# Low rank A of the down projection as extra columns of its weights, and a later place for each tile's last low rank product

## The reference, cut to what matters

```
def _qlinear(x, q, scale, A, Bm):            # I = 1376, H = 512, R = 32
    w = (q.astype(jnp.float32) - 7.5) * (scale * 0.005)[:, None]
    y = jnp.einsum('bsh,oh->bso', x, w)
    return y + 0.02 * (x @ A @ Bm)
g = _qlinear(x, gate_q, gate_scale, gate_A, gate_B)
u = _qlinear(x, up_q, up_scale, up_A, up_B)
h = jax.nn.silu(g) * u
return _qlinear(h, down_q, down_scale, down_A, down_B)   # the map this change is about
```

## Time and profile before

| | |
|---|---|
| device time, three runs | 394.75 us median (393.98 to 395.04) |
| profiled execution | 394.56 us, of which the span of instructions 392.5 us |
| TensorE busy | 381.8 us (97%), 1967 records |
| DVE, ACT, POOL busy | 242.6 us (62%), 174.2 us (44%), 80.2 us (20%) |
| DMA | 40.5 MB, 103 GB/s in the mean |
| chain that ended last | TensorE 86%, DVE 4%, DMA 3%, ACT 3% |
| of it L560; L545; L543 | 37%; 21%; 5% |

### The profile page before, as it was taken

How to read it: one execution, slowest core, us unless ns; L and a number is a source line. 1 busy time by engine, 2 the same in 40 slices (tenths; PEclk the granted TensorE clock), 3 DMA queues, 4 the chain that set the end, 5 groups by cost and what they waited for, 6 DMA issues and landing times.

```text
span 392.5 us, 5221 instructions
## 1 busy us (share of the span) xinstructions
PE 381.8 (97%) x1967; PEld 292.6 (75%) x1968; DVE 242.6 (62%) x370; ACT 174.2 (44%) x307; POOL 80.2 (20%) x67
## 2 busy tenths in 40 slices
PE   8999999999999999999999999999999999999894
PEld 3776787678888876788888767888887778996341
DVE  2649888746376663463766634638889542546994
ACT  6436698312355653123556531235567310575122
POOL 2001433321122232121222321212323312000000
PEclk9899999999999999999999999999999999999999
DMA  7897574199500000072000000860000699790235
GB/s 215 260 287 256 187 225 144 43 343 153 68 1 0 2 0 0 6 116 40 3 0 2 2 0 2 123 142 2 0 0 3 186 291 243 127 224 0 82 135 214
DMA packets 81960, 40.47 MB, mean 103 GB/s; under 512 B 52344, under 2 KB 72840, under 8 KB 81808
## 3 DMA queue, kind: packets, MB, share of 16 engines
q1 hardware_dynamic: 69280, 37.80, 36.7%
q10 hardware_dynamic: 12480, 1.56, 2.9%
q0 software_dynamic: 176, 0.79, 0.7%
HBM read 26.38 MB, written 13.75 MB: 102 GB/s over the span
## 4 chain that ended last, share of the span: by engine, by line
PE 86%; DVE 4%; DMA 3%; ACT 3%; issue 1%; SPq 1%; POOL 0%; DVEq 0%; ACTq 0%
PE ps L560 37%; PE ps L545 21%; PE ps L543 5%; PE ps L570 5%; PE ps L589 4%; PE ps L710 3%; PE ps L505 3%; DMA stage_sel<-in_sel 2%; PE ps L691 2%; PE ps L591 2%; DMA lr_b_rows<-lr_b_parts 1%; PE ps L620 1%; PE ps L519 1%; PE ps L594 1%; PE ps L466 1%
## 5 line engine op out<-in xcount | busy, mean ns | idle before, releaser
L911 POOL TENSOR_TENSOR h_lo<-a_buf,h_hi 128x512 fp32r<-128x512 f32 (+1 forms) x44 | 57.5, 1308 | 143.4 <-ACT h_hi L810 143.4
L560 PE MATMUL ps<-x_hi,gate_w 128*128 128x512 f32 (+1 forms) x176 | 69.8, 397 | 0.1
L560 PE MATMUL ps<-x_hi,up_w 128*128 128x512 f32 (+1 forms) x176 | 69.7, 396 | 0.1
L560 PE MATMUL ps<-x_lo,gate_w 128*128 128x512 f32 (+1 forms) x176 | 69.5, 395 | 0.0
L545 PE MATMUL ps<-down_w,h_hi 128*128 128x512 f32 (+1 forms) x176 | 69.4, 394 | 0.0
L545 PE MATMUL ps<-down_w,h_lo 128*128 128x512 f32 (+1 forms) x176 | 69.3, 394 | 0.0
L560 PE MATMUL ps<-x_lo,up_w 128*128 128x512 f32 (+1 forms) x176 | 69.3, 394 | 0.0
L1155 DVE TENSOR_TENSOR a_buf<-a_buf,b_buf 128x512 f32<-128x512 f32 (+1 forms) x44 | 54.2, 1233 | 11.7 <-ACT a_buf L860 9.8
L846 ACT ACTIVATE a_buf<-ps,gate_sc 128x512 f32<-128x512 f32 (+1 forms) x44 | 30.2, 686 | 27.8 <-POOL h_lo L911 25.5
L1150 DVE TENSOR_TENSOR b_buf<-ps,b_buf 128x512 f32<-128x512 f32 (+1 forms) x44 | 30.1, 685 | 18.7 <-ACT b_buf L849 14.5
L849 ACT ACTIVATE b_buf<-ps,up_sc 128x512 f32<-128x512 f32 (+1 forms) x44 | 30.1, 684 | 23.4 <-PE ps L560 23.3
(11 more groups left out here) (172 smaller groups left out, 491.5 us busy)
## 6 DMA issues: line engine op xcount, KB each, us to landing
x_nat<-in_x SPq DMA_DIRECT2D x4, 1024.0 KB, 7.3
out<-x_nat SPq DMA_DIRECT2D x16, 256.0 KB, 2.3
turned<-x_nat SPq DMA_DIRECT2D x12, 256.0 KB, 3.3
x_nat<-in_down_q SPq DMA_DIRECT2D x11, 256.0 KB, 3.0
x_nat<-in_gate_q SPq DMA_DIRECT2D x10, 256.0 KB, 7.1
x_nat<-in_up_q SPq DMA_DIRECT2D x10, 256.0 KB, 8.4
edges<-zeros SPq DMA_DIRECT2D x4, 512.0 KB, 9.5
xt<-turned SPq DMA_DIRECT2D x6, 256.0 KB, 3.5
```

Source lines behind the costliest of these rows:

```text
L560: last = mm(ps[0:k, bank(ic, 2 * m), :], w[:, H * ic + c * k:H * ic + (c + 1) * k], part[:, c, :], start=c == 0 and part is x1_hi, stop=c ...
L911: nc.gpsimd.tensor_tensor(h_lo[0:k, ic, :], a_buf[0:k, ic % 2, :], plain(h_hi[0:k, ic, :]), ALU.subtract).then_inc(h_lo_ready, 1)
```

## The change

`down_w` gets a second axis: two halves of 256 weight columns, each followed by 32 columns of A, the high part of A in the first half and the low part in the second. Each product of the down map is made twice, once for each half, with 288 moving columns, into two banks: 4 and 5 for even groups, 6 and 7 for odd ones. The products of L543, `down_a_w`, `pd`, the selecting product and the semaphores of these go.

The low rank intermediate now comes out per group, not turned: 128 tokens x 32, in two banks. DVE's `down_scaled` adds both parts in a reduction of 4 x 32 x 2 values (the 32 sums, four times side by side) into `s4`, and then scales the two halves into `y_buf`. `down_turn` turns `s4` on TensorE, a float32 product of 128 columns with the identity, into the odd bank of the pair; ACT (`down_high`) and DVE (`down_low`) split it, scaled, into the group's 128 columns of `t4d`. The low rank product then goes to the even bank of the pair. Both stand in the next group: the turning product at step 2, the low rank one at step 6; in a last group that has the conditioning ahead of it at steps 0 and 8. For a tile's last group the turning product stands behind the next tile's L620 products, the low rank one behind its selecting products (whose banks become 1 and 3 except in tile 0); for the very last group they stand behind convolutions 0 and 1. `down_sum` moves accordingly, and ACT's stores of the last tile stand between its `down_high` steps.

```diff
-        down_w = sb("down_w", [P, IC, H], F32R)
+        down_w = sb("down_w", [P, IC, 2, HALF + R], F32R)
-        pd = sb("pd", [P, TILE], F32R)
+        s4 = sb("s4", [P, 2, P], F32)
...
+        def sel_bank(t, m):
+            return bank(1 if t == 0 else 0, 2 * m + 1)
...
-            def down_repeat(t):
-                pe.wait_ge(pd_hi_ready, t + 1)
-                pe.wait_ge(pd_lo_ready, t + 1)
-                mm(ps[:, 7, :], sel[:], pd[:], start=True, stop=True).then_inc(seld_mm, 1)
+            def down_turn(t, j):
+                n = t * TG + j
+                pe.wait_ge(s4_ready, n + 1)
+                pe.wait_ge(yq_ready, n + 1)
+                mm(ps[:, 5 + 2 * (j % 2), 0:P], s4[:, n % 2, :], ident[:], start=True, stop=True).then_inc(turn_mm, 1)
             def down_low_rank(t, j):
-                if j == 0:
-                    pe.wait_ge(t4d_hi_ready, t + 1)
-                    pe.wait_ge(t4d_lo_ready, t + 1)
-                mm(ps[:, 6 + j % 2, :], t4d[:, j * P:(j + 1) * P], down_b4[:],
+                n = t * TG + j
+                pe.wait_ge(t4d_hi_ready, n + 1)
+                pe.wait_ge(t4d_lo_ready, n + 1)
+                mm(ps[:, 4 + 2 * (j % 2), :], t4d[:, j * P:(j + 1) * P], down_b4[:],
                    start=True, stop=True).then_inc(down_l_mm, 1)
+            def mixed_between(t, j):
+                return j == TG - 1 and t + 1 < TILES
...
-                    if j == 1 and ic == 3:
-                        down_repeat(t)
-                    if j == 1 and ic == 8:
-                        down_low_rank(t, 0)
+                    if j > 0 and ic == (0 if mixed_between(t, j) else 2):
+                        down_turn(t, j - 1)
+                    if j > 0 and ic == (8 if mixed_between(t, j) else 6):
+                        down_low_rank(t, j - 1)
                     for part in (h_hi, h_lo):
-                        if j == 0:
-                            low = mm(ps[0:2 * R, 6, :], down_a_w[0:k, ic].rearrange("p m r -> p (m r)"),
-                                     part[0:k, ic, :], start=first, stop=end)
-                        last = mm(ps[:, 4 + j % 2, :], part[0:k, ic, j * P:(j + 1) * P], down_w[0:k, ic, :],
-                                  start=first, stop=end)
+                        for m in range(2):
+                            last = mm(ps[:, 4 + 2 * (j % 2) + m, 0:HALF + R], part[0:k, ic, j * P:(j + 1) * P],
+                                      down_w[0:k, ic, m, :], start=first, stop=end)
                 last.then_inc(down_mm, 1)
-                if j > 0:
-                    down_low_rank(t, j)
...
+                    if t > 0 and c == HC - 1:
+                        down_turn(t - 1, TG - 1)
...
+                for m in range(2):
+                    mm(ps[:, sel_bank(t, m), :], sel[:], pa[m], start=True, stop=True).then_inc(sel_mm, 1)
                 if t > 0:
-                    pe.wait_ge(y_ready, t * TG)
-                for m in range(2):
-                    mm(ps[:, bank(1, 2 * m + 1), :], sel[:], pa[m], start=True, stop=True).then_inc(sel_mm, 1)
+                    down_low_rank(t - 1, TG - 1)
+                    pe.wait_ge(y_ready, t * TG - 1)
...
                     if t > 0:
+                        if m == 1:
+                            pe.wait_ge(y_ready, t * TG)
                         quantised(t, 1, m)
...
                 convolve(n)
+                if n == 0:
+                    down_turn(TILES - 1, TG - 1)
+                if n == 1:
+                    down_low_rank(TILES - 1, TG - 1)
...
-            def down_high(t):
-                act.wait_ge(seld_mm, t + 1)
-                activation(t4d[:], ps[:, 7, :], copy).then_inc(t4d_hi_ready, 1)
+            def down_high(t, j):
+                n = t * TG + j
+                act.wait_ge(turn_mm, n + 1)
+                activation(t4d[:, j * P:(j + 1) * P], ps[:, 5 + 2 * (j % 2), 0:P], copy,
+                           scale=LR_SCALE).then_inc(t4d_hi_ready, 1)
...
-                for j in range(TG):
-                    if j == 0:
-                        down_high(t)
+                for j in range(TG - 1):
                     if j == 2 and t < TILES - 1:
                         split_mixed(t + 1)
-            for g in range(LATE, GROUPS):
...
+                    down_high(t, j)
+                    if t == TILES - 1 and j > 0:
+                        act.wait_ge(x2_ready, LATE + j)
+                        store(act, LATE + j - 1, stored_late)
+            down_high(TILES - 1, TG - 1)
+            act.wait_ge(x2_ready, GROUPS - 1)
+            store(act, GROUPS - 2, stored_late)
+            act.wait_ge(x2_last, 1)
+            store(act, GROUPS - 1, stored_late)
...
             def down_scaled(t, j):
                 n = t * TG + j
+                x = 4 + 2 * (j % 2)
                 dve.wait_ge(down_mm, n + 1)
                 if n >= 2:
                     dve.wait_ge(x2_ready, n - 1)
-                v.tensor_tensor(y_buf[:, j % 2, :], ps[:, 4 + j % 2, :], down_sb[:], ALU.mult).then_inc(yq_ready, 1)
+                    dve.wait_ge(turn_mm, n - 1)
+                both = ps[:, x:x + 2, HALF:HALF + R].rearrange("p m r -> p r m").unsqueeze(1).to_broadcast([P, P // R, R, 2])
+                v.tensor_reduce(s4[:, n % 2, :].rearrange("p (c r) -> p c r", r=R), both, AX_X, ALU.add).then_inc(s4_ready, 1)
+                v.tensor_tensor(y_buf[:, j % 2, :].rearrange("p (m n) -> p m n", m=2), ps[:, x:x + 2, 0:HALF],
+                                down_sb[:].rearrange("p (m n) -> p m n", m=2), ALU.mult).then_inc(yq_ready, 1)
...
                 if t > 0:
                     x_a_low(t)
+                    down_low(t - 1, TG - 1)
+                    down_sum(t - 1, TG - 1)
```

More of the change, by code:

```diff
@@ L24 @@
 HC = H // P
+HALF = H // 2
 IC = -(-I // P)
@@ L282, in slot, with slot_values @@
             return x_nat[:, GROUPS - RING + n % RING, 0:slot_width(n)].bitcast(I32)
+        def slot_values(n):
+            return slot(n).rearrange("p (m n) -> p m n", m=2) if slots[n][0] == "down" else slot(n)
         def slot_dram(n):
@@ L290, in slot_weights @@
             kind, ic = slots[n]
-            w = {"gate": gate_w[:], "up": up_w[:], "down": down_w[:].rearrange("p c n -> p (c n)")}[kind]
+            if kind == "down":
+                return down_w[:, ic, :, 0:HALF]
+            w = {"gate": gate_w[:], "up": up_w[:]}[kind]
             return w[:, H * ic:H * ic + slot_width(n)]
@@ L778, in down_weights_high @@
                 act.wait_ge(down_in, 3 * 16)
-                activation(down_a_w[:, :, 0, :], stage_down_a[:], copy).then_inc(down_hi, 1)
+                activation(down_w[:, :, 0, HALF:], stage_down_a[:], copy).then_inc(down_hi, 1)
                 activation(down_b4[:], stage_down_b[:], copy).then_inc(down_hi, 1)
@@ L785, in repeated_high @@
                     act.wait_ge(sel_mm, 2 * t + m + 1)
-                    activation(t4[m], ps[:, bank(1, 2 * m + 1), :], copy).then_inc(t4_hi_ready, 1)
+                    activation(t4[m], ps[:, sel_bank(t, m), :], copy).then_inc(t4_hi_ready, 1)
             def convolution_high():
@@ L837, in _ @@
                     x_a_high(t)
+                    down_high(t - 1, TG - 1)
                 else:
@@ L979, in split_mixed @@
                         split_low(t, c - 1)
+                if t > 0:
+                    down_low(t - 1, TG - 2)
                 split_low(t, HC - 1)
@@ L1019, in down_a_low @@
                 dve.wait_ge(down_hi, 1)
-                v.tensor_tensor(down_a_w[:, :, 1, :], stage_down_a[:], plain(down_a_w[:, :, 0, :]), ALU.subtract)
+                v.tensor_tensor(down_w[:, :, 1, HALF:], stage_down_a[:], plain(down_w[:, :, 0, HALF:]), ALU.subtract)
                 dve.wait_ge(down_in, 3 * 16)
@@ L1059, in down_sum @@
                 dve.wait_ge(yq_ready, n + 1)
-                v.tensor_tensor(y_buf[:, j % 2, :], ps[:, 6 + j % 2, :], y_buf[:, j % 2, :],
+                v.tensor_tensor(y_buf[:, j % 2, :], ps[:, 4 + 2 * (j % 2), :], y_buf[:, j % 2, :],
                                 ALU.add).then_inc(y_ready, 1)
@@ L1170, in _ @@
                         convert(later)
-                down_parts_low(t)
                 for j in range(TG):
                     down_scaled(t, j)
-                    if j == 0:
-                        if t == 0:
-                            dve.wait_ge(row_in, 16)
-                        down_low(t)
-                    down_sum(t, j)
+                    if j == 0 and t == 0:
+                        dve.wait_ge(row_in, 16)
                     if j == 2 and t + 1 < TILES:
                         split_mixed(t + 1)
+                    elif j < TG - 1:
+                        down_low(t, j)
+                    if j < TG - 1:
+                        down_sum(t, j)
+            down_low(TILES - 1, TG - 1)
+            down_sum(TILES - 1, TG - 1)
             n = GROUPS - 1
```

35 lines of the change are left out of this document (9 added, 26 removed).

## The result

The changed kernel takes 394.29 us (median of 12 runs, 393.43 to 394.68), the kernel before 395.00 beside it (12 runs, 393.98 to 396.37): a ratio of 0.9977, interval 0.9966 to 0.9988. It is 0.7 us faster, which is inside the 0.3% named as hard to tell from no change, though the interval leaves 1 out, and on the other side of it than forecast: 396.3 had been said, with 394.2 as the cheap end of the likeliest case.

What follows compares the result with a forecast made beforehand. TensorE, busy 97%, was taken to bound the kernel: -4.1 us in the array, +3.5 at turning products, +0.7 in tile 0 and +1.65 at convolution 4 made +1.7, 396.3 us; own range 394.2 to 398.4, wide range 390.6 to 400.2.

Steps and rivals of the forecast that it cites:

- likeliest case: Whole kernel: half width products 132 to 139 ns apart, 394.2 to 398.4 us; chance 0.38.
- Distance of the products: Down map on TensorE: 704 products of 288 columns follow each other at distance c, 135.5 ns, 95.4 us in all.
- The turning product itself: TensorE, s4 against the identity: two records of 112 ns, 0.22 us, sixteen times, 3.6 us.
- Nine waits at turning products: TensorE waits for DVE's y_buf in groups 0 and 1, and the last tile's group 2: 0.385 us each, +3.5 us.
- Tile 0's conversions: Group 0's last step in tile 0 waits for DVE's conversions of down weights: +0.7 us.
- POOL's `h_lo` in tiles 1 to 3: Operand of group 0's last step: slack 0.16 us, no wait unless products come closer than 131.5 ns.
- Convolution 4: TensorE waits 1.65 us for ACT's evacuation 0, which starts 7.7 us after the last down product's start (E).
- A tile's start: Group sum enters DVE's queue ahead of the repeated product's low parts: DVE at most 0.2 us later, no TensorE wait.
- cheap halves: Rival for the down products: excess over the columns in proportion or smaller, 121.5 to 130 ns, 389.3 to 393.2 us; chance 0.32.
- Dear halves: Rival for the down products: weight load collides with moving read, 143 to 148 ns, 400.7 to 403.6 us; chance 0.17.
- a load that isn't hidden: Rival: every half width product waits 0.11 us for its own weight load, 77 us more, about 470; chance 0.01.
- Longer waits: Rival: DVE's reduction takes 0.69 us, or the store before evacuation 0 issues 1.6 later; 397.9 to 400.3 us; chance 0.12.

Runs made afterwards that it cites:

- n64: Changed kernel with 64 of 128 stationary columns in every half width product but each group's first two and last two; 131.7 ns apart, 393.59 us.
- e1: Changed kernel with the turning product of groups 0 and 1 (and 2 in the last tile) at step 3 instead of 2; 391.20 us, ratio to before 0.9904.
- w256: Changed kernel with 256 instead of 288 moving columns in every down product but each half's first; output not the reference's; 389.3 us.
- e2: Changed kernel with ACT's evacuation of convolution 0, and DVE's maximum for it, ahead of the last group's store and sum; 392.57 us, ratio 0.9936.
- e5: Changed kernel with each tile's last low rank product directly behind its turning product, not behind the next tile's selecting products; 405.20 us, ratio 1.0258.
- s1: Kernel before with each down product split into two of 256 columns into the same bank, nothing else; 397.99 us, ratio 1.0055.
- w384: Changed kernel with 384 instead of 288 moving columns in every down product, in two overlapping windows; output not the reference's; 421.0 us.
- w192: Changed kernel with 192 instead of 288 moving columns in every down product but each half's first; output not the reference's; 384.8 us.
- w336: Changed kernel with 336 instead of 288 moving columns in every down product; output not the reference's; 407.1 us.

## Why the prediction was wrong

It named the right mechanisms and the wrong sign, since the sum was a small rest of large terms and one of them was sized 2% too high.

- *Distance of the products.* This is the step that failed. The prediction took "c = 135.5 ns, nearer to the fixed end"; it is 132.4, at the cheap edge of the near range of 132 to 139. 704 x 3.1 ns are 2.2 us, of which the longer waits give back 0.4: 1.8 of the 2.0 between 396.3 and the 394.3 measured. The reason given, that a part of the excess "comes with the load", was read from 0.22 against 0.24 us in two rows of a timeline that is rounded to 0.01; n64 puts the load's part at 0.7 ns with 288 columns. The choice between "fixed" and "in proportion" was also not the whole choice: at 288 columns the excess is 12.4, where proportion gives 10 to 11 and fixed 18. Neither rule holds over the widths tried, and why the excess is 12.4 stays open.
- *The turning product itself*: 0.22 was said. In e1, where it doesn't wait, the third product behind it starts 0.62 behind the last one ahead of it, and three distances are 0.40: 0.22. The number is right and its make-up is not that of two pairs of 0.112: the turning product itself makes 0.14 of it, and 0.08 is a longer distance behind the first down product that follows (0.216 instead of 0.132), seen behind all twelve turning products inside the down map, waited for or not.
- *Nine waits at turning products*: 0.385 each was said, 0.373 measured, and e1 gains them. With c at 132.4 the same working would have given 0.41. Against that, DVE's scaling starts 0.35 behind the reduction's start (155.44 to 155.79), where I had let the reduction's 0.42 pass first, and the 0.07 of the second half hadn't been counted; these two cancel, by luck, and the rest is hundredths in how soon TensorE follows DVE. The reduction itself takes the 0.42 worked out from the values it reads. No wait stands behind the condition, as said.
- *Tile 0's conversions*: 0.7 was said, 0.9 measured, in two waits and not one: the array comes 40 x 3.1 ns = 0.12 earlier to the last step, and the second half's 0.07 hadn't been counted. POOL's `h_lo` in tiles 1 to 3 made no wait at 132.4 and made one in w256, of 0.46 in each tile, where the prediction's working gives 0.48 at 119.4: the slack was sized right.
- *Convolution 4*: 1.65 was said, 1.63 measured, with ACT's evacuation at E + 7.6 where 7.7 was said; e2 shows that the store's place is the cause.
- *A tile's start*: nothing was said, nothing is there. e5 shows what the cover is worth.
- *Sum.* With 132.4 for c and the prediction's own working for the rest (-6.3 in the array, 3.7, 0.8 and 1.65 of waits) the sum would have been about -0.1 instead of +1.7. (The "about 0.08 back" for each nanosecond of c counts the nine waits alone; with tile 0's it is 0.12, as its own rivals have it.) The rivals: cheap halves "decides below c = 132.5", and this is where the chip landed, at the point where it and the forecast meet. Dear halves and a load that isn't hidden are refuted by c. Longer waits didn't come in after, though a long issue of the store, one of the two mechanisms named for them, was seen in e1 (2.86 us) and s1 (4.81).

The Trainium skill's rule for a single warm product, N / 2.4 + 2.5 ns (page "TensorE: Matmul & The Clock Gate", section "Back-to-back issue gap"), would have put c at 122.5. The trace has 132.4, w384 176.0 where the rule gives 162.5, and w192 112.1 where it gives 82.5. For these float32r products the measurement decides against it at every width tried. Of the section "The mechanism" the sentence that a load overlaps only products of other row groups doesn't hold here either: in after's timeline above the loads of L556 at 157.04 begin while the products of 156.83 run, all on the same 128 rows. What the section says of a background weight buffer, into which a load can go ahead, is what this trace looks like.

## What to carry to other kernels

Before an order is changed around the engine that sets the pace, price the product in its new width by a neighbour of nearly that width; a rule for the excess that is fitted to one width moved this sum by more than its result. A product that depends on another engine's answer needs its distance in the queue counted in products: two steps were 0.37 us too few, three were enough, nine times. And an evacuation that a later product waits for doesn't belong behind a store that waits for the slowest chain: moving it ahead gave back 1.7 us.

## What the runs showed of the hardware that was not expected

The distance of float32r products with 128 stationary columns, by moving columns (mean over neighbours):

| moving columns | distance, ns | at 2.4 GHz, ns | excess, ns |
|---|---|---|---|
| 192 (w192) | 112.1 | 80.0 | 32.1 |
| 256 (w256; s1 118.8) | 119.4 | 106.7 | 12.7 |
| 288 (after) | 132.4 | 120.0 | 12.4 |
| 336 (w336) | 153.4 | 140.0 | 13.4 |
| 384 (w384) | 176.0 | 160.0 | 16.0 |
| 512 (before) | 232 to 233.6 | 213.3 | 18.7 to 20.3 |

Between 256 and 336 columns the excess is nearly level, above that it grows with the width, and at 192 the distance is the 112 ns that pairs with 64 and 128 moving columns have too. What makes the excess grow wasn't tried.

A wait of 2.3 us (idle time in the row) in a dense stream of products was followed by products at 1.2 GHz, 427 ns apart instead of 232, in two places of three (e5), at 1.4 to 1.5 us each. The length of the wait alone doesn't decide it: w256 waits 2.8 us at convolution 4, and its clock stays full there. The table by stretch of w256, the wait being 331.2 to 334.1:

```profile
330.00:334.00 4.00, 1.55 (x13) 1.25 (x12) 2.28 (x4) 0.65 (x2) 0.00 (x0) 1.00 1.11 160
334.00:340.00 6.00, 5.91 (x50) 5.85 (x51) 2.07 (x3) 5.26 (x11) 0.00 (x0) 1.00 0.41 108
```

Issuing the same pair of edge DMAs on ACT's queue took between 1.6 and 4.8 us, from one group to the next and from one kernel to another (4.17, 1.71, 1.74 and 1.61 us for the four groups of after), and all of ACT's work behind it waited. What makes it long wasn't tried.
